# Layer 0 attention: the twelve weighing steps of a pair of heads in three blocks of four, not in eight blocks

## What is computed

```python
scores = (einsum('bhqd,bhkd->bhqk', q_nope, k_nope) + einsum('bhqd,bhkd->bhqk', q_pe, k_pe)) * QKD ** (-0.5)
scores = where(mask[:, None], scores, -inf)
attn = softmax(scores, axis=-1)
out = einsum('bhqk,bhkd->bqhd', attn, v).reshape(b, s, H * VD)
return out @ o_w
```

## Time and profile before

| | |
|---|---|
| time, median of 3 runs | 1774.85 us (1766.12 to 1776.11) |
| span of the profiled execution | 1769.7 us |
| PE busy | 1668.8 us, 94% of the span |
| PEld busy | 1226.8 us, 69% |
| DVE busy | 1089.3 us, 62% |
| ACT busy | 849.2 us, 48% |
| POOL busy | 708.5 us, 40% |
| weighing matmuls (L1379) | 768 records, 152.4 us busy, from 563.9 to 1135.3 us |

### The profile page before, as it was taken

One profiled execution on the slowest core, in us unless ns is written; L12 is line 12 of the kernel. 1 busy time (PEld: TensorE's weight loads), 2 busy tenths in 40 slices (PEclk: granted clock), 3 DMA queues, 4 the chain that ended last, 5 costly groups with the idle time before them and its releaser, 6 DMA issues. The chain is left out here.

```text
span 1769.7 us, 27326 instructions
## 1 busy us (share of the span) xinstructions
PE 1668.8 (94%) x8874; PEld 1226.8 (69%) x8874; DVE 1089.3 (62%) x2491; ACT 849.2 (48%) x1595; POOL 708.5 (40%) x735
## 2 busy tenths in 40 slices
PE   6899998999989999999999999789999999999998
PEld 5688887888766666666666666477765555568887
DVE  3556658999747777776777776335657677510222
ACT  3456556443326555555555555344135565653321
POOL 1112213444647566665566665386001111222221
PEclk9999999999999999999999999899979999999999
DMA  7522323220200001000001000364532343131111
GB/s 244 167 73 85 95 84 83 59 66 22 77 13 1 19 19 37 19 19 19 19 19 37 19 19 13 98 203 140 159 48 50 64 81 64 45 98 62 48 48 48
DMA packets 110717, 114.16 MB, mean 65 GB/s; under 512 B 39521, under 2 KB 71745, under 8 KB 110593
## 3 DMA queue, kind: packets, MB, share of 16 engines
q1 hardware_dynamic: 108288, 108.40, 21.8%
q10 hardware_dynamic: 2304, 4.20, 0.6%
HBM read 83.97 MB, written 28.44 MB: 64 GB/s over the span
## 5 line engine op out<-in xcount | busy, mean ns | idle before, releaser
L1490 POOL TENSOR_SCALAR a_p<-a_p,a_rinv 128x640 f32<-128x640 f32 (+7 forms) x256 | 190.6, 748 | 172.6 <-DVE a_rinv L1416 171.6
L1447 ACT ACTIVATE a_p<-a_sm,a_nmax 128x640 f32<-128x640 f32 (+7 forms) x256 | 198.6, 777 | 111.6 <-DVE a_nmax L1408 109.1
L1408 DVE CUSTOM_DVE_ANT_0 a_sm<-ps,maskb 128x640 f32<-128x640 f32 (+7 forms) x256 | 192.5, 752 | 94.7 <-PE ps L1352 91.2
L2334 DVE CUSTOM_DVE_ANT_0 ga_sm<-ps,strip 128x640 f32<-128x640 f32 (+1 forms) x224 | 163.2, 754 | 78.8 <-PE ps L2241 77.3
L2354 ACT ACTIVATE ga_pt<-ps 128x1024 f32<-128x1024 f32 (+1 forms) x192 | 148.1, 810 | 114.8 <-PE ps L2264 114.1
L1364 PE MATMUL ps<-ident,a_p 128*128 128x128 f32 x1152 | 172.1, 274 | 10.6 <-DVE a_pt L1423 10.4
L1364 PEld LDWEIGHTS ps<-ident,a_p 128*128 128x128 f32 x1152 | 132.9, 140 | 33.6 <-issue 10.5
L2394 POOL TENSOR_SCALAR_AFFINE_SELECT ga_pt<-ga_pt 128x512 f32<-128x512 f32 x64 | 40.6, 634 | 286.5 <-ACT ga_pt L2354 286.5
L1379 PE MATMUL ps<-a_pt,vst 128*64 128x512 f32 (+3 forms) x768 | 152.4, 506 | 1.8 <-DVE a_pt L1423 1.1
L1459 ACT COPY a_pt<-ps 128x512 f32<-128x512 f32 x128 | 74.2, 580 | 151.8 <-PE ps L1364 100.0
L1352 PE MATMUL ps<-kh,lq_qh 128*128 128x512 f32 (+3 forms) x384 | 131.7, 397 | 15.4 <-DVE a_nmax L1408 10.6
(11 more groups left out here) (319 smaller groups left out, 3972.1 us busy)
## 6 DMA issues: line engine op xcount, KB each, us to landing
ctx_d<-a_ctxst SPq DMA_DIRECT2D x16, 512.0 KB, 2.9
idx<-ctx_d SPq DMA_DIRECT2D x32, 256.0 KB, 3.8
idx<-wvo_d SPq DMA_DIRECT2D x32, 256.0 KB, 4.5
ga_qst<-qkd SPq DMA_DIRECT2D x42, 128.0 KB, 4.2
f_wr<-in_L_ffn_w SPq DMA_DIRECT2D x18, 256.0 KB, 2.7
x<-in_L_attn_hidden_states SPq DMA_DIRECT2D x16, 256.0 KB, 3.9
op_wo<-in_L_attn_o_w SPq DMA_DIRECT2D x8, 512.0 KB, 4.5
ix_w<-in_L_attn_idx_wq_w SPq DMA_DIRECT2D x64, 64.0 KB, 1.9
```

Source lines behind the costliest of these rows:

```text
L1408: dve.tensor_tensor_reduce(out=sm[kind][:, 0:w], in0=slots[kind][:, 0:w], in1=maskb[:, MASK_OFF[t]:MASK_OFF[t + 1]], scale=-scale, scalar= ...
L1447: act.activation(p[kind][:, v // 2 % 2, 0:w], sm[kind][:, 0:w], ACT.Exp, bias=nmax[:, v % 4:v % 4 + 1], scale=-1.0, accum_out=rsum[:, v % ...
L1490: pool.tensor_scalar(mine, mine, rinv[:, v % 4:v % 4 + 1], 1.0, ALU.mult, ALU.mult).then_inc(norm_done, 1)
L2334: dve.tensor_tensor_reduce(out=sm[kind][:, 0:w], in0=slots[kind][:, 0:w], in1=strip[:, S - w:], scale=-1.0, scalar=3.0e38, op0=ALU.add, op ...
```

## The change

The table `AT` gives the twelve steps in three entries. The steps, their order and their operands stay; what changes is where they stand between the scores and the transposes. In the closing loop a missing entry now means no weighing.

```diff
-        AT = {14: (0, 1), 15: (2, 3), 16: (4,), 17: (5, 6), 18: (7,), 19: (8,), 20: (9, 10), 21: (11,)}
+        AT = {14: (0, 1, 2, 3), 17: (4, 5, 6, 7), 20: (8, 9, 10, 11)}
@@
                 for u in range(NU, 22):
-                    for s in AT[u]:
+                    for s in AT.get(u, ()):
                         weigh(IT - 1, s)
```

## The result

| | before | after |
|---|---|---|
| median of the runs | 1770.63 us (7 runs, 1765.5 to 1777.14) | 1758.63 us (7 runs, 1754.85 to 1761.93) |
| ratio | | 0.9934, 95% interval 0.9912 to 0.9956 |
| span of the profiled execution | 1769.7 us | 1755.6 us |
| start of the last pair's second run of weighing | 1129.73 us | 1116.72 us |
| from one pair to the next | 37.99 us | 37.13 us |

The change gains 0.66%, 12 us by the medians. A second measurement on another occasion gave 0.9936 (0.9913 to 0.9958). Two profiles of the changed kernel gave 37.13 and 37.12 us, so this distance tells differences that the run time can't.

The account below looks back on a forecast made before the run. TensorE was taken to bound the kernel, VectorE next. 75 borders at 0.36 us save 27.0 us, new waits give back 10.0, so 1774.85 - 17.0 = 1757.8, forecast 1758 us; range 1748 to 1770 us.

Parts of the forecast that it names:

- What bounds the kernel: In the changed stage TensorE sets the pace, busy 557.3 of 580 us; VectorE comes next, at 407.4 us.
- Term 1: TensorE's weighing blocks: each costs 0.36 us beside its matmuls, 0.15 inside, 0.18 into it and 0.03 out of it.
- Term 2: Borders removed: five fewer blocks in each of 15 pairs, none in the last pair; 75 blocks, 27.0 us saved.
- Term 3: New TensorE waits for VectorE: 0.32 us at step 1's scores, 0.35 at step 4's single transpose; 10.0 us given back.
- Sum: Whole kernel: 27.0 - 10.0 = 17.0 us gained; span 1752.7 us, median 1758 us after carrying over 5.2 us.
- Nothing given back: Rival, chance 0.12: no new waits for VectorE at steps 1 and 4, so 27.0 us stay gained, 1748 us.
- Twice as much: Rival, chance 0.16: VectorE is late again a step later, 20 us given back, gain 7 us, 1768 us.
- Borders free: Rival, chance 0.04: block borders cost nothing that can be saved, weight loading or drain only displaced; 1775 us.
- Slower through starved VectorE: Rival, chance 0.05: longer blocks leave VectorE without new scores 3.4 us a pair; some 1799 us.
- ScalarE's relief worth nothing: ScalarE's first copy of a pair: the twelfth weighing step comes a step earlier, but TensorE was not waiting; no gain.
- What would show it: Signs in the changed profile: new waits at step 1's scores (`a_nmax`) and step 4's transpose (`a_pt`), pair distance 1.1 us shorter.

Follow-up runs that it names:

- the cut blocks: Kernel before with its four two-step blocks cut in two around the transposes, giving twelve blocks a pair: 39.20 us a pair, 1788.27 us beside 1769.56.
- 128-column run: Kernel before with one 128-column weighing matmul a step replacing two of 64, second head's work left out: 35.69 us a pair, 1729.64 us.
- the runs with one and with two blocks moved: Changed kernel with first block moved to step 15: 36.90 us a pair; with blocks at 15, 18 and 20: 36.46 us, ratio 0.9865.
- a block of eight steps: Kernel before with weighing in two blocks, steps 0-3 at step 15 and 4-11 at step 20: 36.57 us a pair, ratio 0.9862.

## Why the prediction was right, point by point

- **What bounds the kernel** (TensorE, with VectorE next): right. All of the gain and all that was given back lies in TensorE's list against VectorE's results.
- **Term 1, 0.36 us a block**: right in kind, a tenth too large on average. The steps without a wait show 0.33 us, the cut blocks 0.30. At the place where it was read the 0.36 us holds (2.27 against 1.91 us in the 128-column run); the slip was to take the price of one place for that of all. Its cost: 75 x 0.03 = 2 us.
- **Term 2, 75 borders**, none in the last pair: right.
- **Term 3, waits at step 1 and step 4**: both places, both causes and the tie to TensorE's own output were right, as the runs with one and with two blocks moved show. Expected 0.32 and 0.35 us, measured 0.34 (0.37 read directly) and 0.39, and some 0.05 us in the other steps together: 0.8 against 0.67 us, 2 us in all. At step 1 I took 0.06 us from the end of a maximum to the waiting scores; there it was 0.15, and that alone is more than the miss at this place.
- **Sum**: 17.0 us expected, 13 us by the trace, 12 by the medians. Both slips went the same way. That the time itself, 1758.63 against 1758 us, agrees so much better is luck. The runs of the kernel before came out 4 us lower when there were more of them (1770.63 against 1774.85). And the 5.2 us carried over from span to median were mostly spread of the runs: a run's time lies 1.7 us above its own span (1757.35 and 1755.6). The span, forecast at 1752.7 us, came out at 1755.6.
- **Nothing given back**: did not happen, for the reason named. **Twice as much**: no; behind the two places VectorE caught up, and steps 7 to 13 together are unchanged to 0.02 us. **Borders free**: excluded by the twelve blocks and by the 128-column run. **Slower through starved VectorE**: excluded; even a block of eight steps costs nothing of this kind.
- **ScalarE's relief worth nothing**: right, the steps 6 to 13 are not shorter after the change (0.09 us longer).
- **What would show it**: one sign was badly chosen. I looked for the new wait at the scores of step 1 in the view of waits, under `a_nmax`; that row is 6.8 us before and after. The wait exists, but under the modelled end of the transposes.

## What to carry to other kernels

Where a few matmuls with a 64-column operand stand among 128-column ones, count the borders, not only the matmuls: here each block of them cost about a third of a microsecond on the engine that sets the pace. When work is gathered into blocks, ask of every place that it leaves how long before use the other engines' results were there, and whether those results are tied to this engine's own output; moving whole blocks by one step won another 0.67 us a pair, beside the 0.86 us from gathering them. Price such things from start to start and by the distance from one iteration to the next, which here was good to 0.02 us where run times spread over 7 to 12 us.

## What the runs showed of the hardware

- A block of 64-column matmuls among 128-column ones: 0.30 to 0.36 us beside its matmuls; the same block with 128 columns: 0.00 us at the place read (step 3). The weight load for a 64-column block came 0.20 us later after the same eight transposes than that for a 128-column block.
- Two 64-column matmuls side by side took 0.86 us a step at 512 columns, the same as one with 128 columns (5.81 and 5.83 us for the last eight steps), so the two run together.
- From the end of a VectorE or ScalarE operation to the start of the TensorE work that waits for it: 0.15 us at three places (866.82 to 866.97, 877.25 to 877.40, 871.73 to 871.88), 0.14 and 0.06 us at the two of the earlier trace rows.
